# Attention with its side products moved: spread projections, denominators and V in the output's PSUM bank, and a block of probabilities added by a DMA

## What is computed

```python
x_ln = layer_norm(x_flat, g1, beta1)          # 16 images, 1024 positions, 64 channels
q, k, v = split(x_ln @ w_qkv.T)               # 8 heads of 32
scores = einsum('bhqd,bhkd->bhqk', q, k) * 32 ** -0.5
attn = softmax(scores, axis=-1)
out = einsum('bhqk,bhkd->bhqd', attn, v)
```

## Time and profile before

| what | value |
|---|---|
| time, median of 3 runs | 3674.92 us (3674.7 to 3675.24) |
| the profiled execution, first to last instruction | 3666.4 us |
| what lies around that span in a run, by the difference | 8.5 us |
| attention phase in the trace | from about 70 to 1985 us |
| one group of attention, in its even part | 58.18 us |

### The profile page before, as it was taken

The page is one execution under the profiler, slowest core; times in us unless marked ns, Lnnn a source line. Parts: engine busy times, 40 slices in busy tenths (PEclk is TensorE's granted clock), DMA queues, the critical chain, the costliest instruction groups (busy, mean ns, idle before and its releaser), DMA issues. The chain is left out here.

```text
span 3666.4 us, 55668 instructions
## 1 busy us (share of the span) xinstructions
PE 3163.0 (86%) x18550; PEld 1183.9 (32%) x18550; DVE 2573.4 (70%) x3346; ACT 2006.1 (55%) x2381; POOL 2214.4 (60%) x684
## 2 busy tenths in 40 slices
PE   6999999999999999999995899774888888887787
PEld 2333333333333333333331233341322222222222
DVE  5777777777767777777771222142888988988988
ACT  3566666666656666666663333223555564565554
POOL 0577777777777777777776000003657666666666
PEclk7899999999999999999998999886989999999999
DMA  2000000000000000000003211114333433443443
GB/s 103 12 16 10 16 16 16 16 13 16 16 17 10 16 16 16 19 10 16 16 10 74 92 69 46 48 64 149 119 132 128 155 142 120 153 150 118 147 150 115
DMA packets 74739, 234.86 MB, mean 64 GB/s; under 512 B 13088, under 2 KB 14180, under 8 KB 74420
## 3 DMA queue, kind: packets, MB, share of 16 engines
q1 hardware_dynamic: 69460, 215.06, 17.3%
q0 software_dynamic: 5056, 16.83, 1.3%
HBM read 192.42 MB, written 39.39 MB: 63 GB/s over the span
## 5 line engine op out<-in xcount | busy, mean ns | idle before, releaser
L526 DVE TENSOR_REDUCE at_pmax<-at_ring 128x1 f32<-128x512 f32 x2048 | 1300.8, 685 | 392.0 <-PE at_ring L334 381.2
L479 ACT ACTIVATE at_probs<-at_sc 128x1024 f32<-128x1024 f32 x1024 | 992.5, 1021 | 531.7 <-PE at_sc L402 529.7
L580 POOL TENSOR_TENSOR at_prob_sums<-at_prob_sums,at_probs 128x2048 f32<-128x2048 f32 x256 | 1159.0, 4527 | 74.8 <-ACT at_probs L479 54.5
L398 PE MATMUL at_sc<-at_QT,at_KT 32*128 32x512 f32 x4096 | 782.5, 634 | 4.1 <-issue 3.7
L1634 POOL TENSOR_TENSOR ss_drive<-ss_du,ss_bsb 128x1024 f32<-128x1024 f32 x261 | 610.7, 2352 | 263.9 <-DVE ss_state L1591 257.1
L1534 ACT ACTIVATE ss_decay<-ss_delta,ss_a 128x512 f32<-128x512 f32 x520 | 354.5, 687 | 447.6 <-DVE ss_state L1587 299.5
L410 PE MATMUL at_O<-at_probs,at_V 128*32 128x512 f32 x4096 | 535.3, 606 | 52.5 <-DVE at_att L549 51.6
L580 POOL TENSOR_TENSOR at_prob_sums<-at_probs 128x2048 f32<-128x2048 f32 x64 | 290.7, 4543 | 403.1 <-ACT at_probs L479 403.1
L1423 PE MATMUL ss_Y<-ss_seen,ss_ident 128*128 128x512 f32 x1032 | 520.7, 628 | 0.0
L334 PE MATMUL at_ring<-at_KH,at_QH 32*128 32x512 bf16 x2048 | 442.3, 387 | 5.7 <-DVE at_pmax L526 2.9
L1599 DVE TENSOR_TENSOR ss_seen<-ss_state,ss_C 128x1024 f32<-128x1024 f32 x259 | 316.3, 1221 | 80.4 <-PE ss_C L1411 72.6
(11 more groups left out here) (199 smaller groups left out, 2695.6 us busy)
## 6 DMA issues: line engine op xcount, KB each, us to landing
ss_bsb<-scratch_rows SPq DMA_DIRECT2D x265, 512.0 KB, 6.9
scratch_attn<-at_att SPq DMA_DIRECT2D x64, 256.0 KB, 2.0
fc_att<-scratch_attn SPq DMA_DIRECT2D x32, 512.0 KB, 5.8
ss_xn<-scratch_xm SPq DMA_DIRECT2D x34, 256.0 KB, 5.6
at_xn<-scratch_xn SPq DMA_DIRECT2D x32, 256.0 KB, 3.8
ss_xw<-scratch_xw SPq DMA_DIRECT2D x17, 256.0 KB, 3.9
ln_x<-in_x SPq DMA_DIRECT2D x8, 512.0 KB, 4.2
scratch_xn<-ln_xn POOLq DMA_DIRECT2D x8, 512.0 KB, 3.0
```

The lines of the kernel that those rows point to most:

```text
L398: nc.tensor.matmul(sc[:, h, :], KT[head(h), par, blk(kb)], QT[head(h), par, hs(half)], start=True, stop=False)
L479: nc.scalar.activation(probs[:, kb, two, :].rearrange("p h q -> p (h q)"), sc[:, two, :].rearrange("p h q -> p (h q)"), ACT.Exp, scale=SCA ...
L526: nc.vector.tensor_reduce(pmax[:, quad // 2, h, quad % 2:quad % 2 + 1], ring[:, unit[3], :], AX_X, ALU.max, negate=True).then_inc(max_done, 1)
L580: nc.gpsimd.tensor_tensor(prob_sums[:, half, :, :], before, probs[:, k, :, :], ALU.add).then_inc(pool_sums, 1)
```

## The change

Seven things change in the attention phase, and nothing elsewhere.

1. The extras are spread: Q and K projections stand at steps 0, 1, 3 and 9, one at a time, the turned maxima at steps 7 and 15; `LATE` goes from 3 to 5.
2. V and the denominators leave the ring. They are made in `O` between two halves: at a half's step 0 the last product with V, then ACT copies `O` raw into `att`; at step 2 the denominators; at step 3 half of V's projection, which ACT copies out; then the products with V.
3. So the products with V are packed (`PV_AT`): two blocks in each of the half's steps 4, 5 and 6, one in step 7, the last in the next half's step 0.
4. POOL adds blocks 1, 2, 4, 6 and 7 to block 0. Block 5 is added onto block 3 by a DMA that accumulates, from SBUF to SBUF (1 MB), issued by POOL before its addition of block 6. PE then has 2 denominator sources, block 3 and `prob_sums`.
5. DVE's bf16 casts read `QT` and `KT` in SBUF rather than the ring's bank, so a bank that held Q or K is free when ACT has read it.
6. DVE's normalise works on `att` in SBUF, both inputs and the output, and no longer holds `O`.
7. PE's wait for the turned maxima stands after the first two score products of a half, not ahead of them.

```diff
-    LATE = 3
-    SUMMED = 5
+    LATE = 5
+    POOL_ADDS = (1, 2, 4, 6, 7)
+    ONTO, ADDED, ADDED_BEFORE = 3, 5, 6
+    SUMMED = len(POOL_ADDS)
-    extra = {0: [("q", 0), ("k", 0)], 1: [("q", 1), ("k", 1), ("den", 1)], 4: [("turn", 1)], 6: [("v", 0), ("v", 1)],
-             9: [("den", 0)], 12: [("turn", 0)]}
-    MADE_AHEAD = ("q", "k", "v")
+    extra = {0: [("q", 0)], 1: [("k", 0)], 3: [("k", 1)], 7: [("turn", 1)], 9: [("q", 1)], 15: [("turn", 0)]}
+    MADE_AHEAD = ("q", "k")
+    ADDED_AT, SUMS_AT, V_AT = 2, 2, 3
+    LAST_KB = KB - 1
+    PV_AT = {0: (LAST_KB,), 4: (0, 1), 5: (2, 3), 6: (4, 5), 7: (6,)}
...
+            def values_projected(stage, grp, par, half):
...
+                    pe.wait_ge(lden_done, 2 * grp + half)
                 at = 2 * INNER + (1 - par) * P
...
+                rows = slice(half * C, (half + 1) * C)
+                for n in range(KB // 2):
+                    k = half * KB // 2 + n
+                    m = nc.tensor.matmul(O[:, blk(n)], xn[rows, blk(k)], w[rows, at:at + P], start=True, stop=True)
+                m.then_inc(v_ready, 1)
...
-                pe.wait_ge(pool_sums, SUMMED * (2 * (grp - half) + half + 1))
-                srcs = [probs[:, k, :, :] for k in range(SUMMED + 1, KB)] + [prob_sums[:, half, :, :]]
...
+            def denominators_added(of_half):
+                pe.wait_ge(raw_done, of_half + 1)
+                pe.wait_ge(block_added, DMA * (of_half + 1))
+                denominator(probs[:, ONTO, :, :], True, False)
+            def denominators_sums(of_half, half):
+                pe.wait_ge(pool_sums, SUMMED * (of_half + 1))
+                denominator(prob_sums[:, half, :, :], False, True).then_inc(den_ready, 1)
...
-                    pe.wait_ge(od_free, 2 * grp + half)
+                        pe.wait_ge(v_done, v_halves(grp, half))
...
+            def take_raw(grp, half):
+                act.wait_ge(pv_done, STEPS * grp + KB * (half + 1))
...
+                nc.scalar.activation(att[:, half, :], O[:], ACT.Copy).then_inc(raw_done, 1)
...
+                nc.scalar.activation(V[:, 1 - par, half * KB // 2:(half + 1) * KB // 2, :].rearrange("p k d -> p (k d)"), O[:],
+                                     ACT.Copy).then_inc(v_done, 1)
...
-                    nc.vector.tensor_copy(to[:, 1 - par, hs(which)], ring[:, unit[3], :]).then_inc(cast_done, 1)
+                of, to = {"q": (QT, QH), "k": (KT, KH)}[kind]
...
+                nc.vector.tensor_copy(to[:, 1 - par, hs(which)], of[:, 1 - par, hs(which)]).then_inc(cast_done, 1)
...
-                nc.vector.tensor_tensor(att[:, half, :], rden[:], O[:], ALU.mult).then_inc(od_free, 1)
+                nc.vector.tensor_tensor(att[:, half, :], att[:, half, :], rden[:], ALU.mult).then_inc(od_free, 1)
...
-                    for k in range(1, SUMMED + 1):
+                    for n, k in enumerate(POOL_ADDS):
+                        if k == ADDED_BEFORE:
+                            pool.wait_ge(exp_done, 2 * (STEPS * grp + KB * half + ADDED) + 2)
+                            pool.wait_ge(pv_done, STEPS * grp + KB * half + ONTO + 1)
...
+                            pool.dma_start(probs[:, ONTO, :, :], probs[:, ADDED, :, :], accum_op=ALU.add).then_inc(block_added, DMA)
```

More of the change, by code:

```diff
@@ L169, in executed @@
             return ahead
-        if stage == "last":
-            return not ahead
-        return not (stage == "first" and kind == "den" and which == 1)
+        return not ahead if stage == "last" else True
     def period_units(stage):
@@ L335, in maxima, with project @@
                                      start=True, stop=True).then_inc(max_ready, 1)
-            def project(stage, grp, par, half):
-                if not executed(stage, "q", half, 0):
+            def project(stage, grp, par, kind, half):
+                if not executed(stage, kind, half, 0):
                     return
-                if half == 0 and par == 1:
+                if (kind, half) == ("q", 0) and par == 1:
                     pe.wait_ge(xn_in, (grp + 3) * DMA)
[L342 to L348, removed]
@@ L350, in values_projected @@
-            def values_projected(stage, grp, par):
-                if not executed(stage, "v", 0, 6):
-                    return
-                units = [unit_of(stage, "v", n) for n in range(2)]
-                for unit in units:
-                    wait_for_bank(stage, grp, unit)
-                at = 2 * INNER + (1 - par) * P
[L357 to L363, removed]
+                unit = unit_of(stage, kind, half)
@@ new lines, in project @@
+                wait_for_bank(stage, grp, unit)
+                n = "qk".index(kind)
+                rows = slice(n * C, (n + 1) * C)
+                at = n * INNER + (1 - par) * P
+                nc.tensor.matmul(ring[:, unit[3], :], w[rows, at:at + P], xn[rows, hs(half)],
+                                 start=True, stop=True).then_inc(extra_ready, 1)
+            def values_projected(stage, grp, par, half):
+                if stage == "last":
+                    return
+                if stage == "lead" or (stage == "first" and half == 0):
+                    if v_halves(grp, half) > 1:
+                        pe.wait_ge(v_done, v_halves(grp, half) - 1)
+                else:
+                    pe.wait_ge(lden_done, 2 * grp + half)
+                at = 2 * INNER + (1 - par) * P
+                rows = slice(half * C, (half + 1) * C)
[3 more added lines that the diff above has]
+                m.then_inc(v_ready, 1)
@@ L436, in period @@
+                    for kind, which in extra.get(s, []):
+                        if kind == "turn":
+                            turn(stage, grp, which)
+                        else:
+                            project(stage, grp, par, kind, which)
                     maxima(stage, grp, par, s, (2, 3))
                 if stage == "last":
-                    pe.wait_ge(exp_done, 2 * STEPS * NG)
-                    values(grp, par, STEPS - 1)
-                    D = ring[:, 0, :]
-                    pe.wait_ge(max_done, counted_before(N_MAX, grp) + N_MAX["last"])
@@ L469, in period @@
                     half, kb = divmod(s, KB)
+                    closes = stage != "lead" and not (stage == "first" and half == 0)
                     if stage != "lead":
```

184 lines of the change are left out of this document (93 added, 91 removed).

## The result

The changed kernel takes 3795.08 us (median of 3; 3794.89 to 3810.01) against 3674.92: a ratio of 1.034, 95% interval 1.032 to 1.037. It is slower, where 3511 had been forecast, and lies above the range given.

The account below looks back on a forecast made before the run. No engine is full; PE's work and waits in its own order set the 58.18 us group. Work 49.6 plus waits 3.4 makes 53.0, 5.2 less over 31.5 groups: 164 us saved, 3511 us; range 3470 to 3720.

Parts of the forecast that it names:

- the first rival: DVE's casts and normalise, all in SBUF, wait for POOL's running addition: 6.5 us a group, 3716 us; chance 0.25 in full.
- the sum: Attention group: PE's work 49.6 plus waits 3.4 gives 53.0 us, 5.2 less than before; 3511 us; chance 0.42.
- waits of 3.4 a group: PE's waits that stay or come, for DVE, ACT, turns and mixed steps; 3.4 us, bounds 0 and 7.1.
- The prediction's sign for the rival: DVE's casts or normalise would have idle time ahead of them that ends with an addition of POOL.
- the last Q's cast: On DVE, after step 9's exponentials: waits 4.0 us for POOL's addition, and the ring stops PE for 2.9.
- the first K's: K's cast on DVE waits 2.2 us for POOL's addition, costing PE 1.2.
- the first Q's: The first Q's cast on DVE waits 1.2 us for POOL's addition, costing PE 1.2 more.
- the normalises: A group's two normalises on DVE wait 0.8 us each for POOL's addition, costing PE 0.5 and 0.7.
- V's small products: V's eight small products on PE, one row half four at a time: 2.0 us a group, between 1.2 and 2.3.
- The double steps: Steps with two products with V: 3.35 us on PE (1.49 + 1.01 + 0.86).
- The third rival: POOL or the accumulating DMA is late, PE waits in both halves: landing at 16 gives 3795 us; chance 0.10.
- the second rival: DVE's pace made the 7.1 us of waits, so only PE's 1.5 are saved: 3628 us; chance 0.20, including half the blocking.

Follow-up runs that it names:

- 9: idle time filled: The changed kernel with the first four denominator products of each half done three times over on PE; 3704.78 us, ratio 1.009.
- 1: other casts: The changed kernel with its four casts a group written as a maximum over an axis of length one; 3817.26 us, ratio 1.040.
- 5: nothing waits: The changed kernel with casts as maxima over an axis of length one and the normalise moved from DVE to POOL; 3531.78 us, ratio 0.963.
- the sixth kernel: The changed kernel with casts as maxima over an axis of length one and the normalise as a scan with both inputs in SBUF; 3880.26 us, ratio 1.057.
- the third: The changed kernel with POOL's additions cut to one head of four, nothing edited on DVE, PE or ACT; 3514.3 us, ratio 0.958.
- the fourth experiment: The kernel before with only its casts reading Q and K from SBUF, banks free after ACT's copy; 3765.58 us, ratio 1.027.

## Why the prediction was wrong

The mean lengths of the steps that differ, and of the group, worked out from the starts of ACT's exponentials over 28 groups of each trace (us; a few groups are longer than the rest, so a mean lies up to 0.6 above the even group):

| kernel | step 1 | 2 | 3 | 4 | 10 | 11 | 12 | group |
|---|---|---|---|---|---|---|---|---|
| before | 6.13 | 4.24 | 2.68 | 3.55 | 4.25 | 2.68 | 3.55 | 58.5 |
| changed | 3.60 | 5.89 | 4.65 | 3.72 | 5.94 | 3.64 | 4.50 | 62.2 |
| 9: idle time filled | 3.65 | 5.39 | 3.11 | 3.89 | 5.94 | 2.59 | 4.42 | 59.3 |
| 1: other casts | 3.69 | 3.39 | 3.11 | 7.95 | 3.46 | 2.59 | 8.88 | 63.4 |
| 5: nothing waits | 3.76 | 3.54 | 3.11 | 3.51 | 3.46 | 2.59 | 3.93 | 54.1 |

**The step that failed** is the one that set the first rival aside: that the state-space phase's scan, "with two SBUF inputs", ran inside POOL's product in 1.22 us. It does not have two such inputs. The declaration of its tiles reads

```python
aux, decay, Cp, Y = ps("ss_aux"), ps("ss_decay"), ps("ss_C"), ps("ss_Y")
```

so the decay lies in PSUM (`ps` makes a PSUM tile), and the scan has one input in SBUF, `ss_drive`. A row of a profile names the tile and its shape, not its memory; I took the memory for granted. The earlier trace rows said nothing on the question, and the sixth kernel asked it properly. The normalise before, with `O` in PSUM, was the same case. With that evidence gone, no row spoke against the rival. The rule of the Trainium skill that the prediction had set against the scans ("SBUF — State Buffer", section Who interferes with whom) should then have carried it. The runs here agree with it in three parts: casts within SBUF wait (410 to 3870 ns; no run shows in which mode they run), products of two SBUF inputs wait (680 to 3831), and reductions, which that section says never contend on trn2, do not (668 to 686). In the sum the step shows as waits of 3.4 a group in which POOL's additions stood for nothing, and as prices that were all taken at a granted clock of 1.00; the changed kernel loses 5.2 a group to those additions and 2.9 to the clock, as the next paragraph works out. The prediction's sign for the rival, idle time on DVE that ends with an addition of POOL, did not show either: the wait lies inside the durations.

**The rival's mechanism was right, but it had no term for the clock.** It named the last Q's cast, the first K's, the first Q's and the normalises, with 6.5 us a group for PE, a group of 59.5 and 3716. The last Q's and the first K's casts wait, 3.4 and 3.2 us each in every group (4.0 and 2.2 given); the first Q's waits only 0.2 (1.2 given), the normalises 0.7 or less in these groups (0.8 given). Compared with the fifth kernel the changed one loses 8.1 a group (62.2 less 54.1). Of this 5.2 remain when PE's idle time is filled (59.3 less 54.1): those are the waits, 1.3 less than the rival's 6.5. The other 2.9 are the clock, in steps 2, 3 and 11. So the change passes from a gain to a loss: 54.1, 59.3 and 62.2 against 58.5. That the ninth kernel's 59.3 and 3705 lie so near the rival's 59.5 and 3716 is in part luck: its waits were 1.3 too long, and the group to which it added them was 1.1 shorter than the fifth kernel's. The range given reached to 3720 and so held the waits; it is the clock's 2.9 a group, about 90 us, that carried the time out of it.

**Without the waits the sum was about right, in part by luck.** 53.0 was forecast; the third and fifth kernels' even groups take 53.3 and 53.6 (medians). Inside it two terms were off and cancel in part: V's small products take about 1.2 a group, the lower bound, not 2.0 (half of V and one projection, which was priced at 1.0, fill the 1.6 between 760.82 and 762.43 in the fifth kernel's PE timeline), and what is left over for waits is then about 4.8 rather than 3.4. In the changed kernel V's products are slower (a median of 417 ns, against 272 in the fifth and the ninth kernel): steps 3 and 11, in which they stand, are the ones at the low clock. The double steps take 3.35 as forecast.

**POOL and the DMA.** The third rival falls: issue 0.85 (0.6 to 1.1 given), landing 7.0 (8 taken), and its removal makes the fifth kernel slower. **The waits that stay**, the second rival, is no cause of the loss either, since the third and the fifth kernel come near the forecast group. The waits for the ring rise with the casts (345 us to 443.5 in PE's weight loads):

```profile
PEld at_ring L341 <- DVE at_pmax L548: 443.5, 489, 2.9
```

**Left open:** why the low clock follows the same kind of idle time in step 3 of some groups and in step 11 of others (of 28 groups of the changed kernel 13 have it in step 3 alone, 11 in step 11 alone, 4 in both, though PE stands still in steps 2 and 10 of all). The records show the level, the runs show that filling the idle time removes it; what decides between two groups they do not show.

## What to carry to other kernels

Moving an operand from PSUM to SBUF frees a bank, but on DVE it may put the instruction behind an addition that POOL is running: before such a move, list which DVE instructions will be copies within SBUF or have two SBUF inputs, and ask what POOL does at that moment. Look for the wait inside the instruction (the spread between its shortest and longest duration), since it shows as busy time. And look up a tile's memory in its declaration before a row is taken as evidence; the fourth experiment, one small edit of the kernel before, puts the disputed question to the chip directly.

## What the runs showed that I had not expected

- Extra work made a kernel faster: 1.7 us of idle-time filling a half brought 90 us, because PE's stop of 1.54 us was followed by products at a low clock (2.03 us for eight score products against 1.24). PE stands still in the kernel before as well, for up to 0.9 us at a time ahead of its products with V, and there the clock stays at 1.00.
- The same four casts cost 0.67 us as a reduction over one element, with no wait, and 0.41 to 3.9 as a copy: the operation that is faster alone was the slower one beside POOL.
- Removing one wait lengthened the next: with the casts free, the normalise's median went from 1.4 to 3.5 us, and the time did not fall. Either wait by itself cost about as much as both.
